# First block's x turned feature by feature behind dummy transposes; second block's moments issued from ScalarE; wv loaded first; gate sums in four parts

## What is computed

```python
def _layernorm(x, axis=-1, eps=1e-05):
    m = jnp.mean(x, axis=axis, keepdims=True)
    v = jnp.var(x, axis=axis, keepdims=True)
    return (x - m) / jnp.sqrt(v + eps)
...
qp = _phi(proj(Wq, bq))
kp = _phi(proj(Wk, bk))
v = proj(Wv, bv)
...
kv = kv + jnp.einsum('bhd,bhe->bhde', kt, vt)
ksum = ksum + kt
num = jnp.einsum('bhd,bhde->bhe', qt, kv)
den = jnp.einsum('bhd,bhd->bh', qt, ksum)[..., None] + EPS
...
return out @ Wo.T + bo
```

## Time and profile before

| | us |
|---|---|
| median of three runs | 1916.9 |
| the three runs | 1913.78, 1916.9, 1916.97 |
| the profiled execution, its own time | 1916.06 |
| its span, first to last instruction | 1914.3 |
| TensorE busy in it | 1890.7 |
| VectorE / ScalarE / GpSimd busy | 1569.2 / 663.8 / 889.8 |
| mean granted TensorE clock | 0.998 |

### The profile page before, as it was taken

How to read it: one execution, slowest core, us unless ns; L and a number is a source line. 1 busy time by engine, 2 the same in 40 slices (tenths; PEclk the granted TensorE clock), 3 DMA queues, 4 the chain that set the end, 5 groups by cost and what they waited for, 6 DMA issues and landing times.

```text
span 1914.3 us, 60181 instructions
## 1 busy us (share of the span) xinstructions
PE 1890.7 (99%) x25412; PEld 1659.6 (87%) x25412; DVE 1569.2 (82%) x3356; ACT 663.8 (35%) x1298; POOL 889.8 (46%) x981
## 2 busy tenths in 40 slices
PE   7999999999999999999999999999999999999997
PEld 6888888888888888888888888888888888888887
DVE  7888787888879888778878888887888897888888
ACT  4333333323333332333333433333333333323331
POOL 4345554455443554534554445544345553455422
PEclk9999999999999999999999999999999999999999
DMA  6343234333243432343323334333443234333222
GB/s 215 101 128 112 96 106 128 118 118 112 90 127 119 127 121 74 123 125 116 123 89 118 117 112 136 100 98 113 128 128 112 85 114 130 117 117 113 89 73 90
DMA packets 171197, 217.97 MB, mean 114 GB/s; under 512 B 24368, under 2 KB 85808, under 8 KB 170928
## 3 DMA queue, kind: packets, MB, share of 16 engines
q1 hardware_dynamic: 170928, 214.13, 35.4%
HBM read 151.02 MB, written 63.04 MB: 112 GB/s over the span
## 4 chain that ended last, share of the span: by engine, by line
PE 95%; DVE 2%; POOL 1%; DMA 1%; issue 0%; SPq 0%; ACT 0%; POOLq 0%; DVEq 0%
PE ring L684 38%; PE ring L666 36%; PE ring L758 7%; PE num_ps L788 6%; PE num_ps L771 3%; PE num_ps L801 2%; PE ring L730 1%; PE ring L743 1%; DMA v_tok<-in_wv_t 1%; DVE s_mask L973 0%; PE ring L654 0%; DVE stats L1091 0%; DVE den L1220 0%; DVE res L1084 0%; DVE o_lo L1215 0%
## 5 line engine op out<-in xcount | busy, mean ns | idle before, releaser
L1315 POOL TENSOR_TENSOR k_sum<-k_sum,q_raw 128x512 f32<-128x512 f32 x128 | 165.3, 1291 | 545.0 <-DVE q_raw L984 545.0
L883 ACT ACTIVATE e_tmp<-ring,bias_n 128x512 f32<-128x512 f32 x256 | 175.9, 687 | 509.3 <-PE ring L666 508.7
L973 DVE TENSOR_TENSOR s_mask<-ring,causal 128x512 f32<-128x512 f32 x512 | 315.0, 677 | 0.0
L684 PE MATMUL ring<-wv_hi,xt_hi 128*128 128x260 f32 x1024 | 298.9, 292 | 0.0
L684 PE MATMUL ring<-wv_hi,xt_lo 128*128 128x260 f32 x1024 | 289.2, 282 | 0.0
L684 PE MATMUL ring<-wv_lo,xt_hi 128*128 128x260 f32 x1024 | 289.2, 282 | 0.0
L684 PE MATMUL ring<-wo_hi,o_hi 128*128 128x260 f32 x1016 | 284.8, 281 | 1.3 <-ACT o_hi L938 1.3
L684 PE MATMUL ring<-wo_lo,o_hi 128*128 128x260 f32 x1016 | 285.7, 282 | 0.0
L684 PE MATMUL ring<-wo_hi,o_lo 128*128 128x260 f32 x1016 | 285.5, 284 | 0.2 <-DVE o_lo L1215 0.2
L938 ACT ACTIVATE o_hi<-num_ps 128x512 fp32r<-128x512 f32 x127 | 75.8, 597 | 465.9 <-PE num_ps L788 465.9
L666 PE MATMUL ring<-xt_hi,wk_hi 128*128 128x512 f32 x512 | 207.2, 405 | 3.4 <-DVE xt_lo L1042 1.7
(11 more groups left out here) (147 smaller groups left out, 3955.4 us busy)
## 6 DMA issues: line engine op xcount, KB each, us to landing
x_tok<-in_x SPq DMA_DIRECT2D x128, 256.0 KB, 3.8
res<-in_x SPq DMA_DIRECT2D x128, 256.0 KB, 2.8
out<-res SPq DMA_DIRECT2D x128, 256.0 KB, 2.1
x_in<-in_x_t SPq DMA_DIRECT2D x124, 256.0 KB, 4.7
keys_turned<-k_turned SPq DMA_DIRECT2D x112, 256.0 KB, 2.0
k_tok<-keys_turned SPq DMA_DIRECT2D x448, 64.0 KB, 2.1
x_rows<-moments_rows SPq DMA_DIRECT2D x31, 512.0 KB, 3.6
k_t<-in_wk_t SPq DMA_DIRECT2D x4, 256.0 KB, 4.5
```

The lines of the kernel that those rows point to most:

```text
L684: mm = pe.matmul(bank[:, 0:HW], rows[a](k), w[b][:, k, h, :], start=n == 0, stop=n == 3 * KD - 1)
L883: act.activation(e_tmp[:, m], bank, ACT.Relu, bias=bias_n[:, m, g:g + 1], scale=-1.0).then_inc(phi_relu.handle, 1)
L973: dve.tensor_tensor(s_mask[:, j], ring[:, st.bank(u)].rearrange("p (g t) -> p g t", g=KD), repeat(causal, KD), ALU.mult).then_inc(free[st. ...
L1315: pool.tensor_tensor(k_sum[:, g], k_sum[:, g], q_raw[:, g], ALU.mult).then_inc(prod.handle, 1)
```

## The change

1. Step -2, TensorE: behind the statistics of the second tile it does 24 transposes of the identity into bank 0 (`keep_busy`), then turns x, each tile's four pieces into four banks (2 to 5), so that bank 2 + k holds feature group k of all tokens. A bank is reported full with the last tile. ScalarE and VectorE split by feature group.
2. Step -1, TensorE: K0 is done by `project_first`, which takes feature group k once its high part is there, and then waits for its low part; the wait for all low parts is gone.
3. ScalarE and VectorE: the splits of wk and wq are interleaved with the phis (`first_chunks`, `next_chunks`); the bias operations stand ahead of the low parts of x; block 1's statistics stand behind Q0's phi and ahead of K1's; key sums come later; wv is split in two halves, between the phis of c = 1; the operations on constants come behind Q3's phi.
4. Gate sums: one group of 8 instructions behind each of Q2, K3, Q3 and V0.
5. Loads: wk and wq of two column groups ahead of the bias columns; wv_t and wo ahead of `x_in`. wk's stage is now `s_mask`, wq's is the second half of `q_div`.
6. Block 1's moments: written and read back on ScalarE's queue, the write behind Q1's exp, the broadcast behind K2's.
7. GpSimd: reciprocal roots of block 1 first; tile 1 normalised between the products 2 and 3. VectorE: low parts of x of tiles 0 and 1 at c = 2, ahead of `divide`.

The core of the diff:

```diff
+TURN_BANKS = [2 + k for k in range(D // P)]
+WARMING = 24
...
-    stages = {"wk_t": k_t[:, 0], "wq_t": q_raw, "wv_t": v_tok, "wo_t": k_t[:, 1], "wo": q_div[:, 0]}
+    stages = {"wk_t": s_mask.rearrange("p j g t -> p j (g t)"), "wq_t": q_div[:, 1], "wv_t": v_tok, "wo_t": k_t[:, 1], "wo": q_div[:, 0]}
...
-    SPLITS = [(name, g) for g in range(KD) for name in BY_COLUMNS] + [("wv_t", None), ("wo_t", None)]
+    SPLITS = [(name, g) for g in range(KD) for name in BY_COLUMNS] + [("wv_t", 0), ("wv_t", 1), ("wo_t", None)]
...
-                    load_weights(sp, LOADS[:2])
+                    load_weights(sp, LOADS[:4])
                     load_columns(sp)
-                    load_weights(sp, LOADS[2:-3])
+                    load_weights(sp, LOADS[4:-3])
                     load_rows(sp)
                     return
+                load_weights(sp, [("wv_t", None), ("wo", None)])
                 load_features(st)
-                load_weights(sp, LOADS[-3:])
-                spread_moments(st)
+                load_weights(sp, LOADS[-1:])
...
+        def keep_busy():
+
+            pe.wait_ge(x_stat.handle, x_stat.at(2))
+            for _ in range(WARMING):
+                pe.transpose(ring[:, 0, 0:P], ident, ident)
+
         def turn_first(c):
 
-            pe.wait_ge(free[c].handle, free[c].at(0))
             pe.wait_ge(x_normed.handle, x_normed.at(c + 1))
-            for k in range(KD):
-                mm = pe.transpose(ring[:, c, k * P:(k + 1) * P], x_tok[:, c, k * P:(k + 1) * P], ident)
-            mm.then_inc(full[c].handle, 1)
+            for k, b in enumerate(TURN_BANKS):
+                if c == 0:
+                    pe.wait_ge(free[b].handle, free[b].at(0))
+                mm = pe.transpose(ring[:, b, c * P:(c + 1) * P], x_tok[:, c, k * P:(k + 1) * P], ident)
+                if c == TPB - 1:
+                    mm.then_inc(full[b].handle, 1)
+
+        def project_first():
+
+            u = ("K", 0)
+            bank = ring[:, BANK[u]]
+            pe.wait_ge(free[BANK[u]].handle, free[BANK[u]].at(0))
+            pe.wait_ge(ready["wk_t"].handle, 1)
+            for k, b in enumerate(TURN_BANKS):
+                pe.wait_ge(xt_hi.handle, xt_hi.at(k + 1))
+                for a in range(2):
+                    pe.matmul(bank, w_k[a][:, k, 0:P], xt[0][:, k, :], start=k == 0 and a == 0, stop=False)
+                pe.wait_ge(free[b].handle, free[b].at(1))
+                mm = pe.matmul(bank, w_k[0][:, k, 0:P], xt[1][:, k, :], start=False, stop=k == KD - 1)
+            mm.then_inc(full[BANK[u]].handle, 1)
...
+        def first_chunks(st):
+
+            split_high(act, "wk_t", 1)
+            split_high(act, "wq_t", 1)
             act.wait_ge(bias_set.handle, BIASES)
+            relu_exp(st, "K", 0)
+            split_high(act, "wk_t", 2)
+            split_high(act, "wq_t", 2)
+            relu_exp(st, "Q", 0)
+            split_high(act, "wk_t", 3)
+            split_high(act, "wq_t", 3)
+            relu_exp(st, "K", 1)
+            relu_exp(st, "Q", 1)
+            act.wait_ge(x_rstd.handle, x_rstd.at(1))
+            moments_out(act, 1)
+            relu_exp(st, "K", 2)
+            moments_in(act, 1)
+            split_high(act, "wv_t", 0)
+            relu_exp(st, "Q", 2)
+            split_high(act, "wv_t", 1)
+            relu_exp(st, "K", 3)
+            relu_exp(st, "Q", 3)
...
                 split_low(dve, "wk_t", 0)
-                for c in range(TPB):
-                    split_first_low(c)
+                set_biases(dve)
+                for k, b in enumerate(TURN_BANKS):
+                    split_first_low(k, b)
...
+        def first_chunks(st):
+
             split_low(dve, "wq_t", 0)
-            set_biases(dve)
-            for name, g in SPLITS[2:2 * KD]:
-                split_low(dve, name, g)
+            split_low(dve, "wk_t", 1)
+            phi(st, "K", 0)
+            split_low(dve, "wq_t", 1)
+            split_low(dve, "wk_t", 2)
+            phi(st, "Q", 0)
+            split_low(dve, "wq_t", 2)
+            moments(st, range(TPB))
+            phi(st, "K", 1)
+            split_low(dve, "wk_t", 3)
+            phi(st, "Q", 1)
+            split_low(dve, "wq_t", 3)
+            key_sums(st, 0)
+
+        def next_chunks(st):
+
+            phi(st, "K", 2)
+            key_sums(st, 1)
+            phi(st, "Q", 2)
+            key_sums(st, 2)
+            split_low(dve, "wv_t", 0)
+            phi(st, "K", 3)
+            split_low(dve, "wv_t", 1)
+            split_gates(dve, "wv_t", gw.rearrange("p k (h e) -> p k h e", h=2), 0)
+            key_sums(st, 3)
+            phi(st, "Q", 3)
             set_from_constants(dve)
             dve.wait_ge(row_load.handle, ROWS)
...
+                if c == 0 and not attn:
+                    rstds(st)
                 if proj:
                     chunks(st, c, 0, 1)
-                if c == (1 if attn else 0) and turns:
+                if c == 1 and attn and turns:
                     rstds(st)
+                if c == 1 and not attn:
+                    normalise(st, 1)
                 if proj:
                     chunks(st, c, 2, 3)
                 if turns and (c == 2 or not attn and c < 2):
-                    for a in (range(TPB) if attn else ((0,), (1, 2), (3,))[c]):
+                    for a in (range(TPB) if attn else ((0,), (2,), (3,))[c]):
                         normalise(st, a)
```

More of the change, by code:

```diff
@@ L288, in attention @@
     COLS, ROWS, BIASES, CONSTS = 4 * 16, 2 * 16, 3, 19 + E
-    READY = {"wv_t": 2, "wo_t": 4}
+    READY = {"wv_t": 3, "wo_t": 4}
     def halves(ap):
@@ L325, in split_high @@
     def split_high(act, name, g=None):
-        act.wait_ge(w_load[name, g].handle, 16)
+        act.wait_ge(w_load[name, g if name in BY_COLUMNS else None].handle, 16)
         stage, parts = weights(name, g)
@@ L457, in give @@
             eng.sem_inc(s.handle, s.credit)
-    base_m1 = [int(k < TPB) for k in range(NBANK)]
+    base_m1 = [int(k in TURN_BANKS) for k in range(NBANK)]
     base_0 = [a + b for a, b in zip(base_m1, per_bank(("proj", "turn")))]
@@ L524, in load_x @@
             if a == 1:
-                for c in range(TPB):
-                    sp.wait_ge(full[c].handle, full[c].at(1))
+                for k in TURN_BANKS:
+                    sp.wait_ge(full[k].handle, full[k].at(1))
             if a > 1:
@@ L812, in body @@
                 last = c == TPB - 1
-                if proj:
-                    if c == 0 and not attn:
-                        for k in range(TPB):
-                            pe.wait_ge(free[k].handle, free[k].at(1))
-                    elif c == 0:
+                if c == 0 and not attn:
+                    project_first()
+                    chunks(st, c, 1)
+                elif c == 1 and not attn:
+                    chunks(st, c, 0, 1)
+                    sum_gates(pe, (0,))
+                elif proj:
+                    if c == 0:
                         pe.wait_ge(xt_lo.handle, xt_lo.at(TPB * (st.off + 1)))
@@ L828, in body @@
                     from_tile(st, c)
-                if c == 1 and not attn:
-                    sum_gates(pe, (0, 1))
                 if c == 2 and not attn:
+                    sum_gates(pe, (3,))
                     sum_columns(pe)
@@ L840, in body @@
                     spread_reciprocals(st)
-                if proj:
+                if c == 1 and not attn:
+                    for place in range(2, 4):
+                        chunks(st, c, place)
+                        sum_gates(pe, (place - 1,))
+                elif proj:
                     chunks(st, c, 2, 3)
@@ L844, in body @@
                     scores(st, st.off + 1, 0)
-                if c == 1 and not attn:
-                    sum_gates(pe, (2, 3))
                 if attn:
@@ L913, in body @@
             if not attn and not proj:
-                for c in range(TPB):
-                    split_first_high(c)
+                for k, b in enumerate(TURN_BANKS):
+                    split_first_high(k, b)
                 return
@@ L924, in body @@
                     split_x_high(st, 1)
-                if c == 1 and not attn:
-                    split_high(act, "wv_t")
-                if proj:
+                if c == 0 and not attn:
+                    first_chunks(st)
+                elif proj and attn:
                     chunks(st, c, 0, 1)
@@ L950, in body @@
                     act.activation(rden_high, den, ACT.Copy).then_inc(rden_hi.handle, 1)
-                if proj:
+                if proj and attn:
                     chunks(st, c, 2, 3)
@@ L1181, in body @@
                 last = c == TPB - 1
-                if c == 1 and not attn:
-                    split_low(dve, "wv_t")
-                    split_gates(dve, "wv_t", gw.rearrange("p k (h e) -> p k h e", h=2), 0)
                 if c < 2 and attn and proj:
@@ L1192, in body @@
                     residual_moments(st, 2)
-                if proj:
```

(14 more changed lines are left out.)

49 lines of the change are left out of this document (25 added, 24 removed).

## The result

The changed kernel takes 1921.0 us (median of nine runs, 1919.9 to 1921.8) against 1914.2 of the kernel before in the same job (nine runs, 1913.6 to 1917.3): ratio 1.003, 95% interval [1.002, 1.004]. The forecast was 1914.8 and its range ended at 1917.3, so the result is outside, on the side that had a chance of 0.03. By the medians of this job the kernel got 6.8 us slower, where I had forecast a gain of 2.1. The profiled execution took 1920.56 us, 4.5 more than the profiled one before; its span is 1918.9. One execution is not the median: the 33 of the kernel before beside the first experiments lie between 1912.8 and 1920.1.

The account below looks back on a forecast made before the run. TensorE, busy 1890.7 of 1914.3 us, was taken as the bound, so only its idle or slow time could be won. Terms 1.9 + 0.3 - 0.5 + 0.4 = 2.1 us off 1916.9 gave 1914.8, range 1912.0 to 1917.3.

Parts of the forecast that it names:

- Dummies and turning by features: First projections: warmed clock and feature-wise splitting let Q0 start at 16.0, gain 1.9 us.
- the rival in which the clock rises sooner: Head of the run: dummies end before 9.8, K0 ends about 15.1, gain 3.2 us, total 1913.7; chance 0.13.
- Phi ahead of splits: First projections: all phis hidden behind TensorE's work, the wait of 0.3 us goes, gain 0.3.
- Moments on ScalarE: Block 1's moments: the write from ScalarE's queue lands in under 2.5 us, so no wait; gain and loss nil.
- ScalarE stuck on the write: Rival: moments' write lands only at 31.7, V's first matmul comes at 40.9, total 1917.3, slower; chance 0.1.
- wv's chain: Before V's first matmul: VectorE's longer chain of wv splits and gates costs 0.5 us, between 0 and 1.
- GpSimd's order: Block 0's denominators: GpSimd's last product, behind two normalisations, is done by 40.8; no longer wait.
- Low parts of x ahead: Before block 1's first projection: two VectorE copies leave the path, gain 0.4 of the 1.3 us wait.
- a clock below 1.00 in the first projections: Sign of being wrong: TensorE's clock low there, interrupted by waits for low parts; no size given.
- Nothing after 66 us: Loop over the other blocks keeps its instructions and order; any difference there would show the forecast wrong.

Follow-up runs that it names:

- f3: f1 with the loads of x_in and wo_t held until the moments' write has landed; 1918.8 us.
- g1: f3 with the low parts of x of tiles 0 and 1 back behind divide; ratio 0.9994 to the kernel before.
- i2: g1 with GpSimd's first normalisation of block 1 held until wv is split; ratio 0.9998 to the kernel before.
- i3: The kernel of g1 measured once more, nothing changed; ratio 1.0004 to the kernel before.
- e3: The changed kernel without the 24 dummy transposes (WARMING = 0); median 1920.9 us.
- f4: f2 without the dummy transposes; 1918.1 us.
- g3: The kernel before with only the 24 dummy transposes added, behind the second tile's statistics; no measurable difference of the medians.
- e1: The changed kernel with block 1's moments written and read back by SyncE, behind wo_t's load; median 1919.0 us.
- f1: The changed kernel with GpSimd's normalisation of tile 1 behind the third product; worth 0.24 us at block 1, no median stated.
- e2: The changed kernel with 12 dummy transposes before Q3 and 28 before V's first matmul; block 1 starts 2.3 us sooner, no median stated.
- i1: f1 with GpSimd's first normalisation of block 1 held until wv is split; block 1 starts at 63.50, the ratio no better.
- g2: f2 with the low parts of x back behind divide; level with the kernel before.
- f2: The changed kernel with e1's edit and tile 1 normalised behind the third product; 1917.9 us.
- h2: The changed kernel with only the low parts of x back behind divide; block 1 starts 0.9 us later, no median stated.
- h1: g1 with 17 dummy transposes in its small holes (before Q3, V's first matmul and the denominators); ratio 1.0035.

## Why the prediction was wrong

**Dummies and turning by features (forecast: gain 1.9 at Q0's start).** The mechanism was right and the size larger: the clock's records rise at 8.5 us instead of 13.2 (I took 10.4), the transposes run about 0.12 apart (2.03 for sixteen), K0 starts 2.9 us sooner and Q0 2.7 (15.23 against 17.94). That is the rival in which the clock rises sooner. The rule of the Trainium skill, "TensorE: Matmul & The Clock Gate", section "Part 4: PE-mode transpose", that transposes don't count for the clock, is against this trace: nothing but transposes had run when it rose. But the term was added to the end as if no wait lay behind V's start. With the write's delay mended V does start where I had it (37.9; 37.91 in f3, 38.21 in g1, 37.37 in i2), 3 to 4 us before the kernel before, and block 1 then starts 0.1 to 1.0 us sooner at best (g1, i2, i3). No median shows a gain clear of the noise, in these or in the dummies' own runs (e3, f4, g3).

**Phi ahead of splits (gain 0.3).** Right in itself: behind K0's start TensorE has no wait up to 33.56.

**Moments on ScalarE (nil). This is the step that failed.** I read the 4.5 us of the write before as its place on SyncE's queue and took "under 2.5". Measured: 5.9 on ScalarE's queue, 6.4 on SyncE's (e1), 2.4 only with the engines quiet (f3), where V's first matmul comes at 37.91, against 43.19 in f1, the same kernel but for the held loads. The rival "ScalarE stuck on the write", at 0.1, is what happened: it foresaw a landing at 31.7 (it was 31.3), Q2's phi at 35.1 (34.8) and Q3 0.9 late (1.4). The Trainium skill, "DMA: Bandwidth & Descriptors", section "Queues, rings and completion order", says that each DMA engine goes round between the queues that have work, packet by packet. The runs don't bear out what I drew from it, a quick landing for a small write.

**wv's chain (loss 0.5).** The second step that failed. I took halves of 1.15, from the 2.3 of rows 7, and gate operations of 0.35 in all, both as they are with GpSimd idle, and let only the scan stretch. The chain that the stall had delayed by some 3.4 us (Q2's phi at 34.08 against 30.63 in f3) was then 4.1 longer beside GpSimd (2.30 + 1.91 + 1.23 + 1.45 against 2 x 1.22 + 0.17 + 0.19). V came at 43.6, where the rival had 40.9 (its own terms, 35.1 and 5.6, make 40.7). Rows 8 showed the stretch of a scan; whether other operations stretch beside GpSimd I could have looked up in the trace.

**GpSimd's order ("the denominators don't wait longer").** Wrong, but hidden in the changed kernel; e1 uncovers 3.4 us.

**Low parts of x ahead (gain 0.4).** K0' waits 0.84 instead of 1.29, as forecast. It holds only while V is late: in f3 the same place costs 3.6 us (g1).

**The clock.** I named "a clock below 1.00 in the first projections" as a sign of being wrong and gave it no price; it fell later, at the holes before Q3 and V. It cost 2.3 us in the changed kernel (e2). The same kernel can have it or not: g1 ran 3.4 us at 1.2 GHz before block 1, i3 none.

**Nothing after 66 us.** True of the changed kernel: the rest is 1855.4 against 1856.2.

The loss at block 1's first projection, 63.48 - 58.09 = 5.4 us, is thus priced by what each mend gives back there: 2.3 for the clock (e2), 2.75 for ScalarE's stall as far as no other wait takes it (e1). VectorE beside GpSimd is 3.7 us on the chain and nothing at the end (i1). These shares overlap and don't add up, since each mend uncovers the next wait. None of the mended kernels shows the forecast gain of 2.1 us (a ratio of 0.9989) clear of the noise: the intervals of g1 and g2 leave room for it, that of i3, the same kernel as g1, doesn't. Which of its terms would reach the end, no run here separates.

## What to carry to other kernels

A computing engine that waits for its own transfer pays whatever the transfer takes under the load of that moment; look at the DMA share of that stretch, not only at the queue. When work is moved, check what the other engine does in the new place: a 0.2 us operation of VectorE can last as long as GpSimd's running one. And a gain in the middle of a path is worth at its end only what the later waits leave: against f1, f3 brought V forward by 5.3 us and block 1 by 1.7.

## What the runs showed of the hardware that I had not expected

- 4 KB written from ScalarE's queue landed after 5.9 us with the DMA share at 1.05, after 2.4 at 0.17; on SyncE's queue behind two more loads it took 6.4, 8.3 and 5.6 (e1, f2, f4).
- VectorE's CAST of 32 columns took 1.23 (changed) and 0.17 (i1), its subtraction on 32 columns 1.45 and 0.19, with a GpSimd operation beside it and without.
- The clock rose on transposes of the identity alone: at 8.5 us in the changed kernel, with nothing but those from 5.3 on. It fell behind a hole of 1.4 us (Q3) and within one of 3.2 us (V), and stayed at 1.2 GHz for 3.4 and 6.8 us though TensorE had work again. Behind holes of 1.4 to 1.5 us at the same place it stayed at 1.00 in e3, f1, h2 and i1.
- Kernels whose loop is the same code differ in the part behind K0' by up to 8.0 us (1854.4 in e2, 1862.4 in h1, one execution each; without h1 the spread is 3.4), more than the whole change.
